# Causal attention with its operands stacked in two halves of 64 partitions, its matmuls as pairs of 64-row TensorE tiles, and a new merged order of all engines

## The reference

```python
x = layernorm(x + hawk(x));  x = layernorm(x + cross_attention(x, ctx));  x = layernorm(x + ffn0(x))
x = layernorm(x + s6_scan(x)); x = layernorm(x + state_space_cross(x, ctx)); x = layernorm(x + ffn1(x))

def ffn0(x):                       # NH = 16 heads of HD = 8, S = 512
    x = x + mla(rmsnorm(x, w_ln1))
    return x + moe(rmsnorm(x, w_ln2))      # 7 routed experts, top 2, and a shared one
def mla(xn):
    kk, qq = concat(k, rope(k_rope)), concat(q, rope(q_rope))      # (B, S, NH, HD)
    scores = einsum('bqhd,bkhd->bhqk', qq, kk) / sqrt(HD)
    scores = where(causal, scores, finfo.min)
    y = einsum('bhqk,bkhd->bqhd', softmax(scores), v)
    return y.reshape(B, S, H) @ W_o
```

## Time and profile before

| | |
|---|---|
| median of 3 runs | 486.77 us (484.85, 486.77, 487.86) |
| span of the profiled execution | 484.9 us, which is also the only time that it gives |
| PE busy | 413.4 us (85%) |
| PEld busy | 202.0 us (42%) |
| DVE busy | 333.5 us (69%) |
| ACT busy | 293.4 us (61%) |
| POOL busy | 125.2 us (26%) |
| mean granted TensorE clock | 0.927 of full speed |

### The profile page before, as it was taken

The page is one execution under the profiler, slowest core; times in us unless marked ns, Lnnn a source line. Parts: engine busy times, 40 slices in busy tenths (PEclk is TensorE's granted clock), DMA queues, the critical chain, the costliest instruction groups (busy, mean ns, idle before and its releaser), DMA issues.

```text
span 484.9 us, 5925 instructions
## 1 busy us (share of the span) xinstructions
PE 413.4 (85%) x2035; PEld 202.0 (42%) x2035; DVE 333.5 (69%) x616; ACT 293.4 (61%) x508; POOL 125.2 (26%) x129
## 2 busy tenths in 40 slices
PE   5968988888889999999977875557889899999995
PEld 2443533443345554434343221232666544544442
DVE  1386567789969953562799999899977543564454
ACT  4865697526245678889576896456347575652125
POOL 1100000000382029007966667745000200000000
PEclk9999999958789999999997996667989999999999
DMA  8950000564181000005008857979500000501401
GB/s 280 341 153 30 1 2 0 170 90 150 50 191 25 2 4 3 2 15 161 0 18 239 211 168 214 213 206 278 230 0 1 1 0 17 159 1 53 123 0 43
DMA packets 26109, 46.62 MB, mean 96 GB/s; under 512 B 7397, under 2 KB 12742, under 8 KB 24918
## 3 DMA queue, kind: packets, MB, share of 16 engines
q1 hardware_dynamic: 25972, 46.15, 33.6%
q10 hardware_dynamic: 108, 0.10, 0.1%
HBM read 41.13 MB, written 5.01 MB: 95 GB/s over the span
## 4 chain that ended last, share of the span: by engine, by line
PE 58%; DVE 19%; ACT 12%; issue 5%; POOL 3%; DMA 2%; SPq 1%; DVEq 0%; ACTq 0%
ACT AR L1207 7%; DVE AR L1553 7%; PE PS L924 7%; PE PS L956 6%; PE PS L929 5%; PE PS L852 4%; PE PS L838 4%; PE PS L821 3%; ACT L1203 3%; PE PS L688 3%; PE PS L1007 2%; DVE stats L1562 2%; DVE AR L1559 2%; POOL AR L2195 2%; DVE AR L1878 2%
## 5 line engine op out<-in xcount | busy, mean ns | idle before, releaser
L1207 ACT ACTIVATE AR<-PS 128x512 f32<-128x512 f32 (+3 forms) x187 | 98.9, 563 | 103.3 <-PE PS L924 49.5
L1553 DVE TENSOR_TENSOR AR<-PS,AR 128x512 f32<-128x512 f32 (+1 forms) x104 | 69.1, 675 | 49.6 <-PE PS L929 30.4
L2195 POOL TENSOR_TENSOR AR<-AR 128x512 f32<-128x512 f32 (+2 forms) x48 | 52.5, 1101 | 137.3 <-DVE AR L1553 106.7
L1207 ACT ACTIVATE AR<-AR 128x256 f32<-128x256 f32 (+3 forms) x110 | 46.7, 463 | 44.3 <-DVE AR L1553 28.0
L1203 ACT ACT_TABLE_LOAD x42 | 53.9, 1283 | 0.8
L1562 DVE TENSOR_REDUCE stats<-PS 128x1 f32<-128x512 f32 (+4 forms) x88 | 43.6, 521 | 10.3 <-PE PS L762 4.3
L1878 DVE TENSOR_TENSOR_SCAN AR<-PS,AR 128x512 f32<-128x512 f32 x32 | 38.8, 1212 | 1.3 <-ACT PS L1207 0.7
L821 PE MATMUL PS<-RR 97*128 97x512 bf16 (+3 forms) x128 | 34.1, 344 | 4.2 <-DVE stats L1562 3.3
L688 PE MATMUL PS<-AR,W_sq 128*128 128x256 f32 x88 | 27.3, 424 | 10.8 <-ACT AR L1207 6.3
L1553 DVE TENSOR_TENSOR AR<-AR 128x512 f32<-128x512 f32 (+2 forms) x48 | 32.3, 689 | 3.9 <-ACT AR L1207 2.6
L1207 ACT ACTIVATE AR<-PS,W_vec 128x256 f32<-128x256 f32 (+1 forms) x46 | 24.2, 545 | 12.6 <-PE PS L688 4.3
(11 more groups left out here) (241 smaller groups left out, 712.8 us busy)
## 6 DMA issues: line engine op xcount, KB each, us to landing
AR<-scan SPq DMA_DIRECT2D x64, 256.0 KB, 3.9
RR<-in_ffn SPq DMA_DIRECT2D x1, 2688.0 KB, 11.1
RR<-in_ones SPq DMA_DIRECT2D x2, 832.0 KB
RR<-in_ones SPq DMA_DIRECT2D x2, 784.0 KB
RA<-in_moe SPq DMA_DIRECT2D x1, 1539.5 KB, 6.2
AR<-weights SPq DMA_DIRECT2D x6, 256.0 KB, 4.8
W_mla<-in_mla SPq DMA_DIRECT2D x1, 1504.0 KB, 15.9
W_late<-in_late SPq DMA_DIRECT2D x1, 1076.0 KB, 11.5
```

The source lines that it names most:

```text
L1207: nc.scalar.activation(out_, in_, func, bias=bias, scale=scale).then_inc(*done("act", *step))
L1553: nc.vector.tensor_tensor(out_, a, b_, op).then_inc(*done("dve", *step))
L2195: nc.gpsimd.tensor_tensor(out_, a, b_, op).then_inc(*done("pool", *step))
```

## The change

The heads are dealt to two halves of the partitions. Half f of a stack holds 48 rows of products at partitions 64f and up, and for the scores three rows of ones or of the maximum's parts behind them; the rows of zeros are gone, and each stack takes half the columns. Two heads of different halves are multiplied as a pair, by 64-row tiles, into a bank each. The mask is added per tile by matmuls of 64 rows and 64 columns, four for a pair, with the mask as the weights; the blocks that lie crosswise come from a small copy of the masks with its halves exchanged, a new load "turned". The maxima's ring is two pairs in four banks. The scores of a pair use banks 1 and 3, and wait for the second exp of the pair before.

Around it: SP issues two DMAs in place of one for each stack transfer; ACT issues two in place of one for the maxima's rows; the negation of the maxima moves from DVE into ACT's copy (scale -1); the stacks lie in the upper half of `RR`, so that the first half of the angles waits for DVE's a6 instead of a.su39, and the second half for a.su39 instead of b.su39. `TURNS` and `TABLES` are new: 40 table loads instead of 42. On DVE, w2.*, sz and a1 to a6 stand earlier, among the steps of the hawk block, hd.s, r1.0 and q1.0 among a's maxima, r2.0, q2.0 and rQ0.0 between a.nr1 and a.nm1, qQ0.0, rQ1.0 and qQ1.0 among b's maxima. On ACT, s10 and s20 come before b.su34, between a.sl0 and a.sl1; before, they came after b.su39.

```diff
-STACK_DMAS = 3
+STACK_DMAS = {"k": 6, "q": 4}
-MROWS = PRODUCTS * HD + ZROWS
+MROWS = PRODUCTS * HD
+ROWS = 64
-TURN0, TURN1 = len(MAXIMA) // 2 + 6, 4
-HEAD_GROUPS = [slice(0, 4), slice(4, 8), slice(8, NH)]
+TURN0, TURN1 = len(MAXIMA_PE) // 2 + 3, 2
+HEAD_GROUPS = [slice(0, 2), slice(2, 4), slice(4, HEADS)]
...
+        def steps_down(f, c, name):
+            if f == c:
+                return w("bf", name)[ROWS * f:ROWS * f + ROWS, :]
+            at = {"mS": 0, "mT": 128}[name]
+            return turned.bitcast(BF16)[ROWS * f:ROWS * f + ROWS, at:at + 128]
...
-                stacked("k", b, 0, 4, HEAD_GROUPS[0], stack["k", b])
+                for f in range(2):
+                    stacked("k", b, 0, 4, f, HEAD_GROUPS[0], stack["k", b])
...
+            def masked_blocks(rings, masked, name):
+                last = []
+                for c in range(2):
+                    for f, ring in enumerate(rings):
+                        rows_ = slice(ROWS * f, ROWS * f + ROWS)
+                        ones = w("bf", "id")[rows_, rows_]
+                        last.append(mm(blocks(ring, masked)[:, :, ROWS * c:ROWS * c + ROWS], steps_down(f, c, name),
+                                       over(ones, [ROWS, len(masked), ROWS], 1), start=False, stop=(c == 1)))
+                return last[-1]
+
+            def max_pair(b, m):
+                g, u = divmod(m, TWOS)
+                rings = [own(b, 2 * (m % 2) + f) for f in range(2)]
+                if m >= 2:
+                    pe.wait_ge(*after("dve", b, f"mx{m - 2}.1"))
+                segs = ([(0, 3, 0)], [(0, 2, 0), (0, 0, 384)], [(1, 3, 0)], [(1, 2, 0), (1, 0, 384)],
+                        [(0, 1, 0), (1, 1, 256)])[u]
+                for j, qt, c in segs:
+                    n_ = 128 * (qt + 1)
+                    for f, ring in enumerate(rings):
+                        rows_ = slice(ROWS * f, ROWS * f + MROWS)
+                        mm(ring[:, c:c + n_], Qst[b][rows_, 2 * g + j, 128 * qt:128 * qt + 128],
+                           Kst[b][rows_, 2 * g + j, 0:n_], start=(c == 0), stop=False)
+                masked = ([3], [2, 3], [3], [2, 3], [1, 3])[u]
+                masked_blocks(rings, masked, "mT").then_inc(*done("pe", b, f"mx{m}"))
+
+            def score_pair(b, m):
+                g, u = divmod(m, TWOS)
+                rings = [own(b, (1, 3)[f]) for f in range(2)]
+                if m:
+                    pe.wait_ge(*after("act", b, f"su{2 * m - 1}"))
...
+                for j, kb, c in segs:
+                    n_ = T - 128 * kb
+                    for f, ring in enumerate(rings):
+                        rows_ = slice(ROWS * f, ROWS * f + KROWS)
+                        mm(ring[:, c:c + n_], Kst[b][rows_, 2 * g + j, 128 * kb:128 * kb + 128],
+                           Qst[b][rows_, 2 * g + j, 128 * kb:T], start=(c == 0), stop=False)
                 masked = [c // 128 for _, _, c in segs]
+                masked_blocks(rings, masked, "mS").then_inc(*done("pe", b, f"su{m}"))
...
+                    if m == TURN0:
+                        pe.wait_ge(*after("dve", b, f"mx{m - 2}.1"))
                         turn_maxima(b, 0, 3)
                         yield
+                        pe.wait_ge(*after("act", b, "nmt0"))
+                    max_pair(b, m)
                     yield
                 pe.wait_ge(*after("act", b, "nmt0"))
-                pe.wait_ge(*after("dve", b, MAXIMA[-3]))
+                pe.wait_ge(*after("dve", b, MAXIMA[-1]))
...
                     f(wT[b][0:3 * HEADS, :], own(b, i).bitcast(BF16)[0:3 * HEADS, 0:T], ACT.Copy, (b, f"nmt{half}"),
+                      scale=-1.0)
                     act.wait_ge(*after("act", b, f"nmt{half}"))
-                    act.dma_start(Qst[b][MROWS:KROWS, HEADS * half:HEADS * half + HEADS, :], wT[b][0:3 * HEADS, :])\
-                        .then_inc(stack["m", b], 16)
+                    n = 3 * HEADS // 2
+                    for f_ in range(2):
+                        act.dma_start(Qst[b][ROWS * f_ + MROWS:ROWS * f_ + KROWS,
+                                             HEADS // 2 * half:HEADS // 2 * half + HEADS // 2, :],
+                                      wT[b][n * f_:n * f_ + n, :]).then_inc(stack["m", b], 16)
...
-                    ts(hi, mm, -1.0, None, ALU.mult, ALU.bypass, (b, f"nh{half}"))
+                    copy(hi, mm, (b, f"nh{half}"))
-                    stt(res, mm, -1.0, hi, ALU.mult, ALU.subtract, (b, f"nr{half}"))
+                    tt(res, mm, hi, ALU.subtract, (b, f"nr{half}"))
...
-                        pool.wait_ge(*after("pe", 0, f"su{GROUPS * UNITS - 1}"))
+                        pool.wait_ge(*after("dve", "w", "a6"))
...
-                        pool.wait_ge(*after("pe", 1, f"su{GROUPS * UNITS - 1}"))
+                        pool.wait_ge(*after("pe", 0, f"su{GROUPS * TWOS - 1}"))
```

More of the change, by code:

```diff
@@ L83 @@
 _K = list(range(UB1))
-PAIRS = range(NH // 2)
-GROUPS, UNITS = NH // 4, 10
+GROUPS, UNITS, TWOS = NH // 4, 10, 5
 STAGE_ENDS = {3: 0, 7: 1, 9: 2}
@@ L131, in _with @@
     return [*steps[:at], step, *steps[at:]]
-_ATT_PE = [x for n in range(GROUPS * UNITS + LAG)
-           for x in ([f"su{n}"] if n < GROUPS * UNITS else [])
-           + [f"pv{g}.{i}" if kind == "pv" else f"yT{g}" for kind, g, i in attention_events(n)]]
+_ATT_PE = [x for m in range(GROUPS * TWOS + -(-LAG // 2))
+           for x in ([f"su{m}"] if m < GROUPS * TWOS else [])
+           + [f"pv{g}.{i}" if kind == "pv" else f"yT{g}"
+              for n in (2 * m, 2 * m + 1) for kind, g, i in attention_events(n)]]
 _ATT_ACT = [x for n in range(GROUPS * UNITS + LAG)
@@ L336, in build @@
                  ["x0", "x1", "vec", "win", "hawk", "xa0", "sq", "mla", "moe0", "late", "s4d", "dft", "ffn1", "bf", "sel0",
-                  "sel1", "scan", "km", "kr", "tm"]}
+                  "sel1", "scan", "km", "kr", "tm", "turned"]}
         more = {(w, b, n): ctx.enter_context(nc.semaphore(f"more_{w}{b}{n}"))
@@ L807, in blocks @@
                 return grid(ap, 128)[:, which[0]:which[-1] + 1:step or 1, :]
-            def max_unit(b, pair, u):
-                hs = (2 * pair, 2 * pair + 1)
-                n = 5 * pair + "ABCDE".index(u)
-                ring = own(b, n % 3)
-                if n >= 3:
-                    pe.wait_ge(*after("dve", b, f"mx{(n - 3) // 5}.{'ABCDE'[(n - 3) % 5]}"))
-                segs = {"A": [(hs[0], 3, 0)], "B": [(hs[0], 2, 0), (hs[0], 0, 384)],
-                        "C": [(hs[1], 3, 0)], "D": [(hs[1], 2, 0), (hs[1], 0, 384)],
-                        "E": [(hs[0], 1, 0), (hs[1], 1, 256)]}[u]
-                for h, qt, c in segs:
-                    n_ = 128 * (qt + 1)
-                    mm(ring[:, c:c + n_], Qst[b][0:MROWS, h, 128 * qt:128 * qt + 128], Kst[b][0:MROWS, h, 0:n_],
-                       start=(qt, c) == segs[0][1:], stop=False)
-                masked = {"A": [3], "B": [2, 3], "C": [3], "D": [2, 3], "E": [1, 3]}[u]
-                last = mm(blocks(ring, masked), w("bf", "id"), over(w("bf", "mS"), [128, len(masked), 128], 1),
-                          start=False, stop=True)
-                last.then_inc(*done("pe", b, f"mx{pair}.{u}"))
@@ L840, in score_unit @@
                 masked = [c // 128 for _, _, c in segs]
-                mm(blocks(ring, masked), w("bf", "id"), over(w("bf", "mT"), [128, len(masked), 128], 1), start=False,
-                   stop=True).then_inc(*done("pe", b, f"su{n}"))
+                masked_blocks(rings, masked, "mS").then_inc(*done("pe", b, f"su{m}"))
             def values(b, g, stage):
@@ L873, in attention @@
                 pe.wait_ge(*after("dve", b, "q2"))
-                pe.wait_ge(stack["k", b], 16 * STACK_DMAS)
-                pe.wait_ge(stack["q", b], 16 * STACK_DMAS)
-                for n in range(len(MAXIMA)):
-                    pair = n // 5
+                pe.wait_ge(loads["turned"], 16 * 2)
+                pe.wait_ge(stack["k", b], 16 * STACK_DMAS["k"])
+                pe.wait_ge(stack["q", b], 16 * STACK_DMAS["q"])
+                for m in range(len(MAXIMA_PE)):
                     for g, heads in enumerate(HEAD_GROUPS[1:]):
-                        if n == 5 * heads.start // 2:
-                            pe.wait_ge(more["k", b, g], 16)
-                            pe.wait_ge(more["q", b, g], 16)
-                    if n == TURN0:
+                        if m == TWOS * heads.start // 2:
+                            pe.wait_ge(more["k", b, g], 16 * 2)
+                            pe.wait_ge(more["q", b, g], 16 * 2)
+                    if m == TURN0:
+                        pe.wait_ge(*after("dve", b, f"mx{m - 2}.1"))
@@ L898, in attention @@
                         yield
-                    for kind, g, stage in attention_events(n):
-                        (values if kind == "pv" else turn_values)(b, g, stage)
-                        yield
+                    for n in (2 * m, 2 * m + 1):
+                        for kind, g, stage in attention_events(n):
```

(2 more changed lines are left out.)

115 lines of the change are left out of this document (60 added, 55 removed), and 46 rows, old and new, of tables (TABLES, TURNS).

## The result

The changed kernel takes 503.15 us (median of four runs, 499.01 to 504.72) against 485.81 for the kernel before (four runs, 484.39 to 487.86). The ratio is 1.0344, with a 95% interval of 1.0303 to 1.0384: slower by 3.4%. The forecast was 494.5, in a range of 479.5 to 505. The profiled execution has a span of 500.3 us, 15.4 above's execution of 484.9.

A forecast was written before the change was run, and what follows sets the result against it. PE was taken to bound both score stages (B, C), DVE the maxima (A) and scans. Terms +2 - 0.7 + 4.5 + 2 = +7.8 on 484.9 gave 492.7; with 1.9 for timed runs, 494.5, range 479.5 to 505.

The forecast's parts named there:

- What the change takes from PE, and from the overlap: Maxima and scores: pairing saves PE some 24 us, none gain by itself; exps and scores no longer overlap within a batch.
- The gap of 0.58: Scores: ACT's idle time per pair between exps wherever it has no other work; 24 such open gaps.
- the masks' part of 0.04: Scores: extra time per pair for four small mask matmuls per block instead of one, 0.04 us in total.
- A, +2: Batch a's maxima, 103.5 to 141.0: DVE bounds it, new order and split stacks add 2 us, bounds -1 to +5.
- B, -0.7: a's scores with b's maxima, 141.0 to 182.7: 41.0 us along ACT's exps against 41.7, bounds -4.7 to +4.
- C, +4.5: b's scores with a's router and first experts, 182.7 to 221.2: 43.0 us against 38.5, bounds -1.6 and +8.
- The clock, +2: Both score stages: PE, less busy, may run at 1.2 GHz part of the time, lengthening open gaps; +2 us.
- Past 221.2, nothing: After unit 2's expert activation: same work in nearly the same order, so delay is carried to the end, nothing added.
- D: Stage from unit 2's activation to the end of a's experts, 221.2 to 242.5 before; no change of its own forecast.
- the faster one: Rival 1, both score stages: gaps are filled and ACT never waits, 479 to 480; chance 0.17.
- That the tiles don't run side by side: Part of rival 3, scores: row tiles serialise, adding 0.27 to each of 24 open gaps, 6.5 us; rival's chance 0.15.
- The clock's rival: Part of rival 3: clock falls throughout both score stages, +9 instead of +2, 501.5; rival's chance 0.15.

The follow-up runs named there:

- e4_no_mask: The changed kernel without the mask matmuls of the score pairs, so scores of later keys stay unmasked: 502.69 us, ratio 1.0325.
- e3_before_single: The kernel before with one wait changed, so that two score units both wait for the last exp of the two before: 499.12 us, ratio 1.031.
- e6_single_old: The changed kernel's stacks and paired maxima, scores as single 64-row units in two alternating banks, merged order of the kernel before: 494.72 us, ratio 1.0184.
- e2_old_order: The changed kernel's pairs and stacks with the merged order and table loads of the kernel before: 502.2 us, ratio 1.033.
- e9_hybrid: The changed kernel with the order of before up to a's last maximum and from unit 2 of the experts, the new order for the scores: 496.11 us, ratio 1.022.
- e1_halves: The changed kernel with a score pair's two tiles released one by one, each exp waiting only for its own tile: 499.48 us, ratio 1.0321.
- e8_early_b: e6_single_old with b's first two pairs of maxima earlier on PE and a's first score unit waiting only for its own bank's maximum: 490.4 us, ratio 1.0098.
- e10_hybrid_single: e9_hybrid's order with score pairs split into single units in two alternating banks, each released by its own exp: 496.03 us, ratio 1.0208.
- e11_mixed: Changed kernel with alternating single score units, the order of before except for a's scores and b's maxima, and hd.m earlier on DVE: 494.48 us, ratio 1.0148.
- e5_nmt1: The changed kernel with three angle steps on DVE moved behind the split of the second half of a's maxima: 504.88 us, ratio 1.0383.

## Why the prediction was right, and where it was too small

The direction held, and the time lies in the range; the size was half. The sum gave +7.8 on the profiled execution, the profile shows +15.4, and the medians +17.3. Term by term:

**What the change takes from PE, and from the overlap: right.** Pairs run side by side, PE's work falls, and none of it is gain. It falls by less than reckoned: PE is busy 401.3 us over the span instead of 413.4, so 12.1 less where 24 were summed up, with part of the rest at the lower clock. The gap of 0.58 was measured at 0.55 to 0.60, the masks' part of 0.04 at 0.06 to 0.11 (e4_no_mask). That losing the overlap is enough for a loss of this size is shown on a kernel without tiles (e3_before_single, +3.1%), and its return in the order of before is worth some 7.5 us by the medians (e6_single_old against e2_old_order).

**A, +2: the term that failed most, +5.9.** Half of it is DVE's own work: 36.25 us busy against 33.59, where 1.3 to 2.1 were reckoned. The other 3.0 come before a's first maximum. The forecast put the hawk block's order into bounds of -1 to +5 without following it. The rows on DVE show that b's steps ahead of the maximum are late, in the changed kernel

```profile
97.90 0.76 DVE L1588 TENSOR_TENSOR x_in<-PS,AR 128x256 f32<-128x256 f32 x2 [3.71 <-ACT AR L1238]
...
106.26 0.25 DVE L1600 RECIPROCAL stats<-stats 128x16 f32<-128x16 f32 x1
106.43 0.63 DVE L1597 TENSOR_REDUCE stats<-PS 128x1 f32<-128x512 f32 x1
```

and in the kernel before:

```profile
94.97 0.76 DVE L1553 TENSOR_TENSOR x_in<-PS,AR 128x256 f32<-128x256 f32 x2 [1.97 <-ACT AR L1207]
...
103.43 0.63 DVE L1562 TENSOR_REDUCE stats<-PS 128x1 f32<-128x512 f32 x1
```

x_in is the output of b's hawk block, and b's context attention starts from it. From there to a's first maximum it is 8.53 here and 8.46 before, so the 3.0 us lie ahead of it. The timelines show two places. On DVE b's step xn2 stands at 86.59 rather than 82.86, now behind the first product of a's latents, which waits 4.26 for PE; PE starts b's next matmuls, which need xn2, at 87.52 rather than 85.35. And on PE a's values (L819, 1.1 us) now stand between the two halves of the sums of b's norm, where before they came behind both. PE's wait of 2.66 for Vaug, at 105.23, cost nothing: that pair was done at 105.69, before DVE came to it. e2_old_order and e9_hybrid show that nearly all of the 5.9 is the order's: with the tiles and the order of before the last maximum comes at 140.5 and 141.0. No run moved these two places alone.

**B, -0.7: measured +0.8; the mechanism held for most of the stage, with wrong sizes.** The sum went along ACT's exps. Cut to B, the chain that ended last gives PE 18.5 us, DVE 9.4, ACT 8.7 and 5.6 in which the profile shows nothing to wait for; before, PE had 40.0 of the 41.7. It follows DVE's split of a's maxima, with the angle steps in it, up to 152.4, then PE at 1.2 GHz, then a stretch of b's maxima. From 161 on it goes from an exp to the pair that waited for it and back, but for b's maxima from 175 to 178:

```profile
180.04 0.39 PE PS L866 x2
180.43 0.08 PE PS L835 x4
...
181.03 0.60 ACT AR L1238
...
181.68 0.39 PE PS L866 x2
```

That is the round trip that the forecast added up. What it mis-sized is the start: exps go on 8.4 after a's last maximum where 6.8 were reckoned, with r2.0 at 1.58 rather than 0.75. And a second row lies close under it, that of b's maxima on DVE with PE in order between the two, which the forecast counted only as a floor of about 37; in e1_halves it is the row that ends last. In e9_hybrid DVE has 33.98 us in B instead of 36.13 and b's first maximum is done 4 us after a's last, rather than 7; B is then 41.5 with the same pairs. The angle steps that the new order puts into B are work in both rows. e8_early_b moved b's first maximum 2.9 earlier and won 1.0 in B in its profile, so that start alone isn't the whole of it. e1_halves, which shortens the exps' row, has a B 1.2 shorter before DVE's row takes over; no run shortens DVE's alone, so the shares stay open.

**C, +4.5: measured +5.4, not resolved in its causes.** Three kernels with alternating units in the order of before (the kernel before, e6_single_old, e8_early_b) have 38.5, 39.0 and 39.0 there, all at a granted clock of 1.00; with pairs, or single release, in that order it is 46.0 and 45.7 (e2_old_order, e3_before_single). But in the new order alternating units don't help (47.4 against 48.3 in e10_hybrid_single and e9_hybrid). So the lost overlap is a sufficient cause in the one order and not the cause in the other, where the experts' matmuls stand in blocks between b's last pairs. Two limits: e11_mixed has alternating units and the order of before in C and took 43.5, with the fall of the clock that its rows show; and these last two kernels have longer Cs than the changed kernel's 43.9, for which no run with alternating units in its own order exists (e1_halves, with part of the overlap back, has 42.5). The chain in its C gives PE 18.1 us and ACT 17.5, before 29.9 and 7.2.

**The clock, +2: contained in B's and C's numbers.** It was 0.87 and 0.96 there. In B it was at 1.2 GHz for 10.8 us, all at the start; the chain that ended last has 4.5 us of PE in them, and no run separates the clock's price. In C one fall costs 4.5 us (e11_mixed beside e8_early_b), more than the +2 for both stages.

**Past 221.2, nothing: measured +3.3.** The step "the same work in nearly the same order, so a delay there is carried to the end" failed. D is 23.3 instead of 21.3, and between 20.9 and 21.4 in each run with the order of before there. The chain there is ACT's, from the end of unit 2's activation to that of unit 4's: 10.5 us here, 8.8 before. b.yt and b.f1.sqa now stand between units 3 and 4, and unit 3 waits longer for PE. ACT's timeline in the changed kernel (unit 3 and b.yt are at 236.34, b.f1.sqa at 241.50, unit 4 at 243.21)

```profile
236.34 1.09 ACT L1238 ACTIVATE AR<-PS 128x512 f32<-128x512 f32 x2 [0.64 <-PE PS L955]
...
241.50 0.40 ACT L1238 ACTIVATE AR<-AR 128x256 f32<-128x256 f32 x1
...
243.21 0.60 ACT L1238 ACTIVATE AR<-PS 128x512 f32<-128x512 f32 x1
```

and in the kernel before (unit 3 at 223.34, unit 4 and then b.yt at 229.42):

```profile
223.34 0.60 ACT L1207 ACTIVATE AR<-PS 128x512 f32<-128x512 f32 x1 [0.24 <-PE PS L924]
...
229.42 1.08 ACT L1207 ACTIVATE AR<-PS 128x512 f32<-128x512 f32 x2
```

No run moved these two steps alone.

The last 1.3 lie within what E varies by between the profiles.

Of the rivals, the faster one is excluded: PE was released in every run with tiles, and none was faster than before. That the tiles don't run side by side is excluded by the row at 105.23. The clock's rival happened in part, for some 14 of 86 us in B and C. The rule from the Trainium skill ("TensorEngine Tiling (Array Packing)", section "PSUM Bottleneck"), that tiling speeds up TensorE but not the emptying of PSUM, went the right way: of the chain in B, ACT's exps and DVE's maxima, both emptying PSUM, now have 8.7 and some 4 us, where PE had 40.0 of 41.7. It speaks of throughput, though, and ACT is busy for only 25.17 of the 42.5 us; what costs time in these rows is that a pair takes both banks at once.

What stays open: how the new order's C splits between the experts' blocks and the clock; which of the two rows in B costs how much; and why e6_single_old's B is 3.5 us longer than before although PE and ACT have no more to do there and DVE only 0.7 us more (its first 5.6 us are at 1.2 GHz, its first score waits for the last maximum, and b's first maximum is done 7.0 after a's last rather than 5.0). e8_early_b, the best version with the new stacks, is still 1.0% over the kernel before.

## What to carry to other kernels

Before halving an engine's time per item, count the buffers that an item takes: two banks that held two items in turn hold one pair, and the engine and its consumer then alternate. A busy share of 98% doesn't say that the engine alone sets a stage: here DVE's row and ACT's exps stood close behind, and work moved onto DVE (the angle steps) went into stages that DVE then helped to bound. When a written-out order changes with an edit, follow it to the first late step in each stage; about half of the loss here, A's 5.9 and D's 2.0 of 15.4 us, was the order's.

## What the runs showed of the hardware

The granted clock can fall in one of two executions of the same sequence: the instructions of e8_early_b and e11_mixed in C are the same, with the same waits, up to the microsecond in which one falls to 1.2 GHz for some 10 us (207.1 to 217.3) and the other stays at full speed. That one fall cost 4.5 us of a stage of 39, and a comparison of single profiles in such stages is uncertain by as much; what decides it, no run here shows.

Some DVE instructions took twice as long and more while POOL wrote its angle tables. In the changed kernel POOL is busy from 143.32 to 149.40. DVE's timeline has a cast of the maxima's split and r2.0 (the multiplication with W_vec) in that time, and instructions of the same shape behind it:

```profile
146.95 0.48 DVE L1603 CAST parts<-stats 128x32 bf16<-128x32 f32 x1
...
148.38 1.58 DVE L1591 TENSOR_SCALAR RR<-RR,W_vec 128x1024 f32<-128x1024 f32 x1
...
151.33 0.75 DVE L1591 TENSOR_SCALAR RR<-RR,W_vec 128x1024 f32<-128x1024 f32 x1
152.00 0.17 DVE L1603 CAST parts<-stats 128x32 bf16<-128x32 f32 x1
```

The cast takes 0.48 beside POOL and 0.17 behind it, the multiplication 1.58 and 0.75. In e5_nmt1 r2.0 itself stands at 149.11, behind the end of POOL's tables at 148.93, and takes 0.75. The maxima, which read PSUM, stay at 0.68. In the kernel before, the 1.52 of r1.0 at 182.60 also lies beside POOL's tables, so the forecast's two prices for r1.0, 0.75 and 1.52, were these two cases. The Trainium skill ("GPSIMD Engine Reference", section "Specifications") says that POOL shares its SBUF interfaces with VectorE and contends with some of its instructions; these rows agree, though no run here had POOL's work taken away.
